# The last clamp of the hidden activation taken from ScalarE to VectorE in a state-space and quantized-FFN layer

## The chip, the cores and the metric

The kernel runs on one Trainium2 chip, on all 8 cores. Every core gets 2 of the 16 sequences (8192 tokens) and works alone: no data passes between cores. The metric is the device time in microseconds of the slowest core.

In the text, PE is TensorE, DVE is VectorE, ACT is ScalarE, SP is the engine that issues most DMAs, and PEld is the weight load that goes with each matmul.

## The reference

One layer: `x = layernorm(x + ssm(x))`, then `x = layernorm(x + ffn(x))`, with x of 16 x 4096 x 1024. The change concerns the FFN, whose activations and weights are rounded to fixed point. Cut to what matters:

```python
def fixed_quant(x, width, frac_width):
    scale = 2.0 ** frac_width
    return clip(round(x * scale), -2**(width-1), 2**(width-1) - 1) / scale
def quantized_relu(x):
    return relu(fixed_quant(x, 8, 4))
h = einsum(fixed_quant(x, 8, 4), fixed_quant(w1, 8, 6)) + fixed_quant(b1, 8, 6)
h = quantized_relu(h)            # 4096 hidden values of each token
out = einsum(fixed_quant(h, 8, 4), fixed_quant(w2, 8, 6)) + fixed_quant(b2, 8, 6)
```

The hidden value is thus scaled by 16, rounded, cut at 127 from above and at 0 from below.

## The kernel before, in words

The program has two phases, written out by hand in one function, `build_nc`. `op`, `wait` and `dma` append instructions to the list of one engine; each engine runs its list in order, and waits on counting semaphores: `tm` counts PE's finished groups, `vd` DVE's instructions, `sd` ACT's. `mm_group` emits one accumulating chain of matmuls into the next of 8 PSUM banks, taken in turn; if the bank's last reader is not done, PE waits for it there. All of a group's matmuls but the last carry line 209, the last carries line 206.

Phase A (lines 291 to 438) is the state-space layer, in 16 blocks of 512 tokens; its result goes to the DRAM tensor `r1s`. Then the FFN weights are loaded and quantized (lines 447 to 479).

Phase B (line 566 on) is the first layernorm, the FFN and the second layernorm, in 32 blocks of 256 tokens, as a software pipeline over three blocks. Iteration `it` does, in the order of each engine's list:

- for block t1 = it + 1, sums over the 1024 features of the input and of its squares on PE (lines 579 to 583). The squares, `sqb1`, were made on ACT (`emit_sq1`, line 509) at the end of the iteration before. `sqb1` lies in the same memory as `htmp8b`, so ACT waits until DVE is through with `htmp8b` (line 505), and behind its own `hq_sb` writes (line 506). `rows_and_s` (lines 518 to 537) makes mean and reciprocal deviation from the sums.
- for block t3 = it - 1, the second FFN matmul: 8 groups of 32 matmuls from `hq_sb` and `w2q`. Each group waits for the last write of `hq_sb` (line 595), and DVE adds bias and residual (line 597). Then ACT makes the squares `sqb2` (line 609), and PE sums them.
- for block t1, DVE applies the layernorm (lines 555 and 561) and quantizes to `xq_sb` (lines 636, 641, 647).
- for block t2 = it, the hidden loop (lines 682 to 723), of which the change is a part. It has 8 steps (`gsub`). In each, PE runs 4 groups of 8 matmuls (`w1q` with `xq_sb`, 128 hidden rows each). DVE makes three passes of 4 instructions over `htmp8b`, a buffer of 4 x 256 fp32 values that exists once: line 696 adds the bias, multiplies by 16 and frees the PSUM bank, line 703 rounds, line 710 takes the minimum with 127. Then ACT applies Relu in 4 instructions (line 718) and writes `hq_sb` in bf16. `prev_htmp_v` and `prev_htmp_s` hold the last DVE and ACT user of `htmp8b`; line 696 of the next step waits for both (lines 690 and 691).
- for block t3, DVE applies the second layernorm (lines 555 and 561 with `ob`), SP stores the result.

In the loop it thus reads, for one step:

```python
wait("V", "vd", prev_htmp_v[0], selfdep=True)
wait("V", "sd", prev_htmp_s[0])
...
wait("S", "vd", v)
...
prev_htmp_s[0] = hq_sd
```

Of the kernel before, what the change touches and what calls it, by code (L numbers as in the profile page):

```python
# [9 lines left out]
AF = mybir.ActivationFunctionType  # L10
ALU = mybir.AluOpType
# [23 lines left out]
def build_nc(debug=False):  # L35
# [90 lines left out]
    hq_sb = sb("hq_sb", [128, HC, TB], BF16, "B")  # L126
    r2_sb = sb("r2_sb", [128, DC, TB], BF16, "B")
    ob = sb("ob", [128, DC, TB], F32, "B")
    htmp8b = sb("htmp8b", [128, 4, TB], F32, "B")
# [16 lines left out]
    with contextlib.ExitStack() as st:  # L146
# [14 lines left out]
        def wait(eng, sem, val, force=False, selfdep=False):  # L161
            if val is None or val <= 0:
                return
            if not force and not selfdep and own_sem.get(eng) == sem:
                return
            if not force and waited[eng].get(sem, 0) >= val:
                return
            waited[eng][sem] = max(waited[eng].get(sem, 0), val)
            emit(eng, lambda E, s=sems[sem], v=val: E.wait_ge(s, v))  # L169
# [4 lines left out]
        def op(eng, fn, inc=None, inck=1):  # L174
            if inc is None:
                emit(eng, fn)
                return None
            cnt[inc] += inck
            emit(eng, lambda E, f=fn, s=sems[inc], k=inck: f(E).then_inc(s, k))
            return cnt[inc]  # L180
# [40 lines left out]
        def dma(eng, q, out_ap, in_ap, pre=()):  # L221
            for s_name, v in pre:
# [24 lines left out]
                                          scalar1=RATE_EPS, scalar2=-1.0,  # L247
                                          op0=ALU.add, op1=ALU.mult), inc="vd")
# [42 lines left out]
        for it in range(NTA + 1):  # L291
            t = it
            tp = it - 1
            if t < NTA:
# [12 lines left out]
                for e in range(8):  # L307
# [5 lines left out]
                        out=u_bf[:, p, e, :], in_=full(b)), inc="sd")  # L313
                    free_bank(b, "sd", sv)
                    u_copy_done = sv
                if debug and t == 0:
# [8 lines left out]
                    out=e1_t[:], in_=full(b), func=AF.Exp,  # L325
# [4 lines left out]
                    out=sp_t[:], in_=e1_t[:], func=AF.Ln, bias=cb_one[:]), inc="sd")  # L330
# [3 lines left out]
                    out=ld_t[:], in0=sp_t[:], scalar1=DT_MAX, scalar2=negrate[:],  # L334
                    op0=ALU.min, op1=ALU.mult), inc="vd")
                wait("S", "vd", vv)
                sv = op("S", lambda E, p=par: E.activation(
                    out=dec_t[:, p, :], in_=ld_t[:], func=AF.Exp), inc="sd")
                wait("V", "sd", sv)
                omd_vv = op("V", lambda E, p=par: E.tensor_scalar(  # L340
                    out=omd_t[:], in0=dec_t[:, p, :], scalar1=1.0, scalar2=-1.0,
                    op0=ALU.subtract, op1=ALU.mult), inc="vd")
# [3 lines left out]
                    out=c_t[:], in0=omd_t[:], in1=full(b), op=ALU.mult), inc="vd")  # L346
# [4 lines left out]
                else:  # L351
                    init = h_t[:, (t - 1) % 2, TA - 1:TA]
                scan_vd[t] = op("V", lambda E, p=par, i=init: E.tensor_tensor_scan(
                    out=h_t[:, p, :], data0=dec_t[:, p, :], data1=c_t[:],
# [3 lines left out]
                    out=hb_t[:, p, :], in_=h_t[:, p, :]), inc="vd")  # L358
# [141 lines left out]
        prev_htmp_s = [0]  # L500
# [65 lines left out]
        for it in range(-1, NTB + 1):  # L566
# [19 lines left out]
            if do3:  # L586
                p3 = t3 % 2
                st3 = state[t3]
                r2_vd = None
                mm2_groups = []  # L590
                for e in range(DC):
                    mlist = [(w2q[:, k, e * 128:(e + 1) * 128], hq_sb[:, k, :])
                             for k in range(HC)]
                    b, tv = mm_group(mlist, lambda bb: ln_slice(bb, TB),
                                     pre_waits=[("sd", st3["hq_sd"])])
                    wait("V", "tm", tv)
                    r2_vd = op("V", lambda E, b=b, e=e, p=p3: E.scalar_tensor_tensor(  # L597
                        out=r2_sb[:, e, :], in0=ln_slice(b, TB),
                        scalar=b2q[:, e:e + 1], in1=x1_sb[:, p, e, :],
                        op0=ALU.add, op1=ALU.add), inc="vd")  # L600
                    free_bank(b, "vd", r2_vd)
                    if e == 3 and do1:
                        bmb1, brs1, tvrs1 = emit_bcasts(rows1, rows1_vd, sv1)
                if not do1:
                    pass
                wait("S", "vd", r2_vd)
                sq2v = None
                for c in range(DC):
                    sq2v = op("S", lambda E, c=c: E.activation(  # L609
                        out=sqb2[:, c, :], in_=r2_sb[:, c, :], func=AF.Square),  # L610
                        inc="sd")
                bm2, tvm2 = mm_group([(ones_bf[:], r2_sb[:, c, :]) for c in range(DC)],
                                     lambda b: row_slice(b, TB),
                                     pre_waits=[("vd", r2_vd)])
                bv2, tvv2 = mm_group([(ones_bf[:], sqb2[:, c, :]) for c in range(DC)],
                                     lambda b: row_slice(b, TB),
                                     pre_waits=[("sd", sq2v)])
            elif do1:
                bmb1, brs1, tvrs1 = emit_bcasts(rows1, rows1_vd, sv1)
# [42 lines left out]
            def emit_ln2_apply(bcasts):  # L662
                bmb2, brs2, tvrs2 = bcasts
                if t3 >= 1 and out_store[t3 - 1] is not None:
                    wait("V", "qo", out_store[t3 - 1])
                src2 = [r2_sb[:, c, :] for c in range(DC)]
                dst2 = [ob[:, c, :] for c in range(DC)]
                apply2_vd = emit_apply(src2, dst2, bmb2, brs2, tvrs2)
                if debug and t3 == 0:
                    dma("Y", "qd", dbg["hq0"].rearrange("(c p) t -> p c t", p=128),  # L670
                        hq_sb[:, :, :], pre=[("sd", st3["hq_sd"])])
                colp = slice(t3 * TB, (t3 + 1) * TB)
                dstap = outT.rearrange("(c p) t -> p c t", p=128)[:, :, colp]
                out_store[t3] = dma("Y", "qo", dstap, ob[:, :, :],
                                    pre=[("vd", apply2_vd)])
# [3 lines left out]
            if do2:  # L679
                p2 = t2 % 2  # L680
                hq_vd = None
                for gsub in range(HC // 4):
                    groups = []
                    for j in range(4):
                        hc = gsub * 4 + j
                        mlist = [(w1q[:, k, hc * 128:(hc + 1) * 128],
                                  xq_sb[:, p2, k, :]) for k in range(DC)]
                        groups.append(mm_group(mlist, lambda bb: ln_slice(bb, TB),
                                               pre_waits=[("vd", state[t2]["xq_vd"])]))
                    wait("V", "vd", prev_htmp_v[0], selfdep=True)  # L690
                    wait("V", "sd", prev_htmp_s[0])
                    for j in range(4):
                        b, tv = groups[j]
                        hc = gsub * 4 + j
                        wait("V", "tm", tv)
                        v = op("V", lambda E, b=b, hc=hc, j=j: E.tensor_scalar(  # L696
                            out=htmp8b[:, j, :], in0=ln_slice(b, TB),
                            scalar1=b1q16[:, hc:hc + 1], scalar2=16.0,
                            op0=ALU.add, op1=ALU.mult), inc="vd")
                        free_bank(b, "vd", v)  # L700
                    wait("V", "vd", v, selfdep=True)
                    for j in range(4):
                        v = op("V", lambda E, j=j: E.tensor_scalar(  # L703
                            out=htmp8b[:, j, :], in0=htmp8b[:, j, :],
                            scalar1=MAGIC, scalar2=MAGIC,
                            op0=ALU.add, op1=ALU.subtract), inc="vd")
                    prev_htmp_v[0] = v
                    wait("V", "vd", v, selfdep=True)
                    for j in range(4):
                        v = op("V", lambda E, j=j: E.tensor_scalar(  # L710
                            out=htmp8b[:, j, :], in0=htmp8b[:, j, :],
                            scalar1=127.0, scalar2=None,
                            op0=ALU.min, op1=ALU.bypass), inc="vd")
                    prev_htmp_v[0] = v
                    wait("S", "vd", v)
                    for j in range(4):
                        hc = gsub * 4 + j
                        hq_sd = op("S", lambda E, j=j, hc=hc: E.activation(  # L718
                            out=hq_sb[:, hc, :], in_=htmp8b[:, j, :],
                            func=AF.Relu), inc="sd")  # L720
                    prev_htmp_s[0] = hq_sd
                    if gsub == 6 and do3:
                        ln2_bcasts = emit_ln2_rows()
                state[t2]["hq_sd"] = hq_sd
                if do3:
                    emit_ln2_apply(ln2_bcasts)
            if 0 <= it + 2 < NTB and "sq1_sd" not in state[it + 2]:
# [87 lines left out]
```

How the kernel before makes its waits and increments, by code:

```python
        def wait(eng, sem, val, force=False, selfdep=False):  # L161
            if val is None or val <= 0:
                return
            if not force and not selfdep and own_sem.get(eng) == sem:
                return
            if not force and waited[eng].get(sem, 0) >= val:
                return
            waited[eng][sem] = max(waited[eng].get(sem, 0), val)
            emit(eng, lambda E, s=sems[sem], v=val: E.wait_ge(s, v))
# [4 lines left out]
        def op(eng, fn, inc=None, inck=1):  # L174
            if inc is None:
                emit(eng, fn)
                return None
            cnt[inc] += inck
            emit(eng, lambda E, f=fn, s=sems[inc], k=inck: f(E).then_inc(s, k))
            return cnt[inc]
```

## Time and profile before

| | us |
|---|---|
| two timed runs | 3930.99 and 4051.89 |
| their median | 3991.44 |
| profiled execution | 3932.01 |
| its span on the slowest core (core 2) | 3930.4 |
| spans of the 8 cores | 3920.2 to 3930.4 |
| mean granted TensorE clock, by core | 0.905 to 0.909 of full |

The profile is one execution, read on its slowest core; the span runs from its first to its last instruction. Durations of instructions are means or single cases from it. On an engine instructions overlap: the next one starts before the end of the last, so the time that a row of the timeline gives for x4 is less than four times the mean of one.

### The profile page before, as it was taken

The page shows a single profiled execution, that of the slowest core. Times are in us where ns is not written, and L with a number is a line of the kernel's source. Part 1 is how long each engine was busy: PE and PEld are TensorE (multiplying, and loading weights), DVE is VectorE, ACT ScalarE, POOL GpSimd, SP SyncE. Part 2 cuts the span into 40 slices and gives each one's busy share as a digit, 9 for nine tenths or more (in the row PEclk, how much of TensorE's full clock was granted, in tenths as well). Part 3 has the DMA queues.
Part 4 walks back from the last instruction along what each step waited for, and adds up shares of the span by engine and source line. Part 5 has one row for each costly group of instructions (what it writes and reads, how often), then busy time and mean ns, then how long its engine had stood idle before and what let it go on. Part 6 is the DMA issues. An engine that isn't in the chain of part 4 may idle for free.

```text
span 3930.4 us, 56360 instructions; the slowest of 8 cores (3920.2 to 3930.4 us)
## 1 busy us (share of the span) xinstructions
PE 2965.1 (75%) x21120; PEld 2102.0 (53%) x21120; DVE 2016.3 (51%) x5836; ACT 786.7 (20%) x2003; POOL 19.0 (0%) x26
## 2 busy tenths in 40 slices
PE   3999999940577777777777777777777777677777
PEld 1444444410466656656555566665666666556665
DVE  0444333358555555555555555555555555555554
ACT  1222222300211121211211211112121211221111
POOL 0000000000000000000000000000000000000000
PEclk9999999975689999899988899999999988988998
DMA  7133322136000000000000000000000000000000
GB/s 105 32 47 46 47 45 43 33 118 245 22 17 17 17 17 23 17 17 17 17 17 17 22 23 17 17 17 17 22 17 17 17 17 17 17 28 17 12 12 22
DMA packets 109820, 128.16 MB, mean 33 GB/s; under 512 B 3936, under 2 KB 102240, under 8 KB 108528
## 3 DMA queue, kind: packets, MB, share of 16 engines
q1 hardware_dynamic: 71936, 83.89, 6.6%
q0 software_dynamic: 20976, 23.89, 5.1%
q10 hardware_dynamic: 16640, 16.78, 1.6%
q8 instruction: 172, 2.82, 0.3%
q14 instruction: 96, 0.79, 0.1%
HBM read 98.07 MB, written 50.33 MB: 38 GB/s over the span
## 4 chain that ended last, share of the span: by engine, by line
PE 47%; DVE 32%; ACT 11%; issue 6%; DMA 2%; another core or an unknown queue 2%; DVEq 1%; ACTq 0%; SPq 0%
PE pb L209 42%; DVE htmp8b L696 8%; ACT hq_sb L718 8%; DVE htmp8b L703 6%; DVE htmp8b L710 6%; PE pb L206 5%; DVE x_sb L561 2%; DVE x_sb L555 2%; ACT sqb L509 2%; DVE htmp8b L636 1%; DVE htmp8b L641 1%; DVE xq_sb L647 1%; DVEq L169 1%; DMA wstage_a<-w1T 1%
## 5 line engine op out<-in xcount | busy, mean ns | idle before, releaser
L209 PE MATMUL pb<-xq_sb,w1q 128*128 128x256 bf16 x7168 | 973.1, 284 | 299.6 <-DVE htmp8b L696 240.5
L209 PEld LDWEIGHTS pb<-xq_sb,w1q 128*128 128x128 bf16 x7168 | 705.4, 101 | 486.3 <-issue 384.2
L209 PE MATMUL pb<-hq_sb,w2q 128*128 128x256 bf16 x7936 | 945.3, 281 | 14.3 <-ACT hq_sb L718 14.3
L209 PEld LDWEIGHTS pb<-hq_sb,w2q 128*128 128x128 bf16 x7936 | 794.3, 101 | 150.6 <-issue 37.9
L696 DVE TENSOR_SCALAR htmp8b<-pb,b1q 128x256 f32<-128x256 f32 x1024 | 424.6, 475 | 362.4 <-ACT hq_sb L718 350.6
L597 DVE SCALAR_TENSOR_TENSOR r_sb<-pb,b2q,x_sb 128x256 bf16<-128x256 f32 x256 | 123.7, 483 | 844.2 <-PE pb L206 844.2
L718 ACT ACTIVATE hq_sb<-htmp8b 128x256 bf16<-128x256 f32 x1024 | 341.5, 404 | 987.1 <-DVE htmp8b L710 987.1
L209 PE MATMUL pb<-xb,winT_sb 128*128 128x512 bf16 x1792 | 431.0, 381 | 61.4 <-DMA xb<-xT 61.4
L209 PE MATMUL pb<-sqb,ones_bf 128*1 128x256 bf16 x448 | 96.5, 385 | 329.9 <-ACT sqb L509 278.2
L209 PEld LDWEIGHTS pb<-xb,winT_sb 128*128 128x128 bf16 x1792 | 175.0, 98 | 275.4 <-issue 69.0
L206 PE MATMUL pb<-xq_sb,w1q 128*128 128x256 bf16 x1024 | 290.4, 284 | 0.0
L609 ACT ACTIVATE sqb<-r_sb 128x256 bf16<-128x256 bf16 x256 | 81.9, 402 | 946.3 <-DVE r_sb L597 946.3
L710 DVE TENSOR_SCALAR htmp8b<-htmp8b 128x256 f32<-128x256 f32 x1024 | 230.5, 288 | 29.1 <-DVE htmp8b L703 1.8
L703 DVE TENSOR_SCALAR htmp8b<-htmp8b 128x256 f32<-128x256 f32 x1024 | 230.3, 288 | 28.5 <-DVE htmp8b L696 1.4
L209 PEld LDWEIGHTS pb<-sqb,ones_bf 128*1 128x1 bf16 x448 | 45.1, 107 | 371.6 <-issue 348.3
L209 PE MATMUL pb<-z_sb,woutT_sb 128*128 128x512 bf16 x896 | 217.0, 383 | 9.5 <-DVE z_sb L420 9.5
L388 DVE TENSOR_TENSOR r_sb<-pb,xb 128x512 bf16<-128x512 f32 x128 | 88.5, 691 | 244.5 <-PE pb L206 244.5
L209 PEld LDWEIGHTS pb<-z_sb,woutT_sb 128*128 128x128 bf16 x896 | 88.1, 98 | 117.5 <-issue 13.3
L312 ACT CAST u_bf<-pb 128x512 bf16<-128x512 f32 x128 | 74.9, 585 | 377.7 <-PE pb L206 377.7
L209 PE MATMUL pb<-r1ld,ones_bf 128*1 128x256 bf16 x224 | 36.4, 313 | 149.1 <-DMA r1ld<-r1s 147.3
L509 ACT ACTIVATE sqb<-r1ld 128x256 bf16<-128x256 bf16 x256 | 81.9, 402 | 204.5 <-DMA r1ld<-r1s 188.4
L206 PE MATMUL pb<-row,ones_row 1*128 1x256 f32 x256 | 80.2, 434 | 53.6 <-DVE htmp8b L696 50.2
(88 smaller groups left out, 1834.9 us busy)
## 6 DMA issues: line engine op xcount, KB each, us to landing
outT<-ob SPq DMA_DIRECT2D x32, 1024.0 KB, 4.4
xb<-xT POOLq DMA_DIRECT2D x16, 1024.0 KB, 16.1
r1s<-r_sb ACTq DMA_DIRECT2D x16, 1024.0 KB, 8.4
r1ld<-r1s SPq DMA_DIRECT2D x32, 512.0 KB, 4.2
wstage_a<-w1T SPq DMA_DIRECT2D x4, 2048.0 KB, 9.3
wstage_b<-w1T SPq DMA_DIRECT2D x4, 2048.0 KB, 9.5
wstage_a<-w2T SPq DMA_DIRECT2D x4, 2048.0 KB, 8.6
wstage_b<-w2T SPq DMA_DIRECT2D x4, 2048.0 KB, 8.5
```

The source lines that it names most:

```text
L206: E.matmul(o, l, r, **kw), inc="tm")
L209: E.matmul(o, l, r, **kw))
L388: vv = op("V", lambda E, b=b, e=e, p=parp, xp=tp % 3: E.tensor_tensor(out=r1_sb[:, p, e, :], in0=full(b), in1=xb[:, xp, e, :], op=ALU.add) ...
L509: sqv = op("S", lambda E, c=c, p=p: E.activation(out=sqb1[:, c, :], in_=r1ld[:, p, c, :], func=AF.Square), inc="sd")
L555: E.tensor_tensor(out=d, in0=s, in1=ln_slice(b, TB), op=ALU.subtract), inc="vd")
L561: E.tensor_tensor(out=d, in0=d, in1=ln_slice(b, TB), op=ALU.mult), inc="vd")
L597: r2_vd = op("V", lambda E, b=b, e=e, p=p3: E.scalar_tensor_tensor(out=r2_sb[:, e, :], in0=ln_slice(b, TB), scalar=b2q[:, e:e + 1], in1=x1 ...
L609: sq2v = op("S", lambda E, c=c: E.activation(out=sqb2[:, c, :], in_=r2_sb[:, c, :], func=AF.Square), inc="sd")
L696: v = op("V", lambda E, b=b, hc=hc, j=j: E.tensor_scalar(out=htmp8b[:, j, :], in0=ln_slice(b, TB), scalar1=b1q16[:, hc:hc + 1], scalar2=16 ...
L703: v = op("V", lambda E, j=j: E.tensor_scalar(out=htmp8b[:, j, :], in0=htmp8b[:, j, :], scalar1=MAGIC, scalar2=MAGIC, op0=ALU.add, op1=ALU. ...
L710: v = op("V", lambda E, j=j: E.tensor_scalar(out=htmp8b[:, j, :], in0=htmp8b[:, j, :], scalar1=127.0, scalar2=None, op0=ALU.min, op1=ALU.b ...
L718: hq_sd = op("S", lambda E, j=j, hc=hc: E.activation(out=hq_sb[:, hc, :], in_=htmp8b[:, j, :], func=AF.Relu), inc="sd")
```

## The change

The four Relu instructions on ACT (line 718) are gone from every step. DVE's third pass, which took the minimum with 127 in place in `htmp8b`, now takes the minimum with 127 and the maximum with 0 in one instruction and writes `hq_sb` in bf16. `prev_htmp_s` is no longer set in the loop, so that it holds the last `sqb1` write. The second FFN matmul waits for DVE's count in place of ACT's.

```diff
-                                     pre_waits=[("sd", st3["hq_sd"])])
+                                     pre_waits=[("vd", st3["hq_vd"])])
...
                     for j in range(4):
-                        v = op("V", lambda E, j=j: E.tensor_scalar(
-                            out=htmp8b[:, j, :], in0=htmp8b[:, j, :],
-                            scalar1=127.0, scalar2=None,
-                            op0=ALU.min, op1=ALU.bypass), inc="vd")
+                        hc = gsub * 4 + j
+                        v = op("V", lambda E, j=j, hc=hc: E.tensor_scalar(
+                            out=hq_sb[:, hc, :], in0=htmp8b[:, j, :],
+                            scalar1=127.0, scalar2=0.0,
+                            op0=ALU.min, op1=ALU.max), inc="vd")
+                    hq_sd = None
                     prev_htmp_v[0] = v
-                    wait("S", "vd", v)
-                    for j in range(4):
-                        hc = gsub * 4 + j
-                        hq_sd = op("S", lambda E, j=j, hc=hc: E.activation(
-                            out=hq_sb[:, hc, :], in_=htmp8b[:, j, :],
-                            func=AF.Relu), inc="sd")
-                    prev_htmp_s[0] = hq_sd
...
-                state[t2]["hq_sd"] = hq_sd
+                state[t2]["hq_vd"] = v
```

DVE's list at the last two steps of a hidden loop and the sums behind it, before; `pb` is a PSUM bank, `b1q` the bias, `row` a row of layernorm sums:

```order
L696 TENSOR_SCALAR htmp8b<-pb,b1q_47 128x256 x4
L703 TENSOR_SCALAR htmp8b<-htmp8b 128x256 x4
L710 TENSOR_SCALAR htmp8b<-htmp8b 128x256 x4
L518 TENSOR_SCALAR row_0_53<-pb 1x256
L523 TENSOR_TENSOR row_1_54<-row_0_53 1x256
```

The same place with the change:

```order
L696 TENSOR_SCALAR htmp8b<-pb,b1q_47 128x256 x4
L703 TENSOR_SCALAR htmp8b<-htmp8b 128x256 x4
L711 TENSOR_SCALAR hq_sb<-htmp8b 128x256 x4
L518 TENSOR_SCALAR row_0_53<-pb 1x256
L523 TENSOR_TENSOR row_1_54<-row_0_53 1x256
```

DVE has as many instructions as before, in the same order; the third pass has another output.

ACT's list from one hidden loop to the next, before; `sqb_89` is `sqb1`, `sqb_90` is `sqb2`:

```order
L718 ACTIVATE hq_sb<-htmp8b 128x256 x32
L509 ACTIVATE sqb_89<-r1ld 128x256 x8
L534 ACTIVATE row_1_54<-row_2_55,cb_eps 1x256
L537 ACTIVATE row_3_56<-row_1_54 1x256
L609 ACTIVATE sqb_90<-r_sb 128x256 x8
L534 ACTIVATE row_1_58<-row_2_59,cb_eps 1x256
L537 ACTIVATE row_3_60<-row_1_58 1x256
```

And with the change:

```order
L509 ACTIVATE sqb_89<-r1ld 128x256 x8
L534 ACTIVATE row_1_54<-row_2_55,cb_eps 1x256
L537 ACTIVATE row_3_56<-row_1_54 1x256
L609 ACTIVATE sqb_90<-r_sb 128x256 x8
L534 ACTIVATE row_1_58<-row_2_59,cb_eps 1x256
L537 ACTIVATE row_3_60<-row_1_58 1x256
```

The 32 Relu instructions of each block are gone; the rest of ACT's list stands in the same order.

## Rows read from the trace of the kernel before

**Rows 1.** The page: busy time of each engine.

```profile
PE 2965.1 (75%) x21120; PEld 2102.0 (53%) x21120; DVE 2016.3 (51%) x5836; ACT 786.7 (20%) x2003; POOL 19.0 (0%) x26
```

**Rows 2.** Waits: engine, line, whom it waited for, us in total, times, longest.

```profile
DVE htmp8b L696 <- ACT hq_sb L718: 350.6, 218, 2.0
...
PE pb L209 <- ACT sqb L509: 278.2, 32, 12.8
...
PE pb L209 <- DVE htmp8b L696: 242.3, 151, 3.2
...
PE pb L209 <- ACT hq_sb L718: 14.3, 2, 8.0
```

**Rows 3.** Timeline of one hidden-loop step: start, us, engine, instructions [idle before].

```profile
2034.88 1.66 DVE L696 TENSOR_SCALAR htmp8b<-pb,b1q 128x256 f32<-128x256 f32 x4 [1.60 <-ACT hq_sb L718]
...
2035.51 0.92 PE L209 MATMUL pb<-xq_sb,w1q 128*128 128x256 bf16 x7 [1.13 <-DVE htmp8b L696]
...
2036.64 0.90 DVE L703 TENSOR_SCALAR htmp8b<-htmp8b 128x256 f32<-128x256 f32 x4
...
2037.65 0.90 DVE L710 TENSOR_SCALAR htmp8b<-htmp8b 128x256 f32<-128x256 f32 x4
...
2038.64 1.33 ACT L718 ACTIVATE hq_sb<-htmp8b 128x256 bf16<-128x256 f32 x4 [3.94 <-DVE htmp8b L710]
...
2038.89 0.27 PE L206 MATMUL pb<-xq_sb,w1q 128*128 128x256 bf16 x1
2040.15 1.66 DVE L696 TENSOR_SCALAR htmp8b<-pb,b1q 128x256 f32<-128x256 f32 x4 [1.60 <-ACT hq_sb L718]
```

**Rows 4.** Timeline of the same block: its last step, and PE until the second matmul.

```profile
2065.90 0.42 PE L206 MATMUL pb<-r1ld,ones_bf 128*1 128x256 bf16 x1
...
2069.57 0.90 DVE L710 TENSOR_SCALAR htmp8b<-htmp8b 128x256 f32<-128x256 f32 x4
...
2070.56 1.33 ACT L718 ACTIVATE hq_sb<-htmp8b 128x256 bf16<-128x256 f32 x4 [3.94 <-DVE htmp8b L710]
2071.98 2.56 ACT L509 ACTIVATE sqb<-r1ld 128x256 bf16<-128x256 bf16 x8
2073.21 2.74 DVE L561 TENSOR_TENSOR ob<-ob,pb 128x256 f32<-128x256 f32 x8
...
2074.68 1.65 PE L209 MATMUL pb<-sqb,ones_bf 128*1 128x256 bf16 x7 [8.37 <-ACT sqb L509]
...
2076.48 5.51 PE L209 MATMUL pb<-hq_sb,w2q 128*128 128x256 bf16 x31
```

**Rows 5.** Timeline: a second-matmul group at full rate, and the one behind it.

```profile
2081.94 3.55 PE L209 MATMUL pb<-hq_sb,w2q 128*128 128x256 bf16 x31
...
2085.43 3.55 PE L209 MATMUL pb<-hq_sb,w2q 128*128 128x256 bf16 x31
```

**Rows 6.** Groups by line and form: busy, mean ns of one, idle before.

```profile
L718 ACT ACTIVATE hq_sb<-htmp8b 128x256 bf16<-128x256 f32 x1024 | 341.5, 404 | 987.1 <-DVE htmp8b L710 987.1
L710 DVE TENSOR_SCALAR htmp8b<-htmp8b 128x256 f32<-128x256 f32 x1024 | 230.5, 288 | 29.1 <-DVE htmp8b L703 1.8
...
L647 DVE TENSOR_SCALAR xq_sb<-htmp8b 128x256 bf16<-128x256 f32 x256 | 57.5, 288 | 6.8
```

**Rows 7.** Timeline: one pass of line 647, into bf16.

```profile
2024.43 0.90 DVE L647 TENSOR_SCALAR xq_sb<-htmp8b 128x256 bf16<-128x256 f32 x4
```

**Rows 8.** Windows: stretch, length, busy us of each engine (instructions), granted clock, DMA share, GB/s.

```profile
100.00:600.00 500.00, 490.96 (x2268) 220.41 (x2267) 200.65 (x307) 149.08 (x227) 8.74 (x10) 1.00 0.28 43
1300.00:3900.00 2600.00, 1964.59 (x15790) 1573.36 (x15789) 1423.64 (x4722) 501.89 (x1480) 0.00 (x0) 0.91 0.06 18
...
2021.00:2063.00 42.00, 30.23 (x254) 24.56 (x253) 29.90 (x107) 8.93 (x26) 0.00 (x0) 0.98 0.05 14
2063.00:2075.00 12.00, 3.63 (x20) 1.93 (x19) 9.87 (x35) 5.22 (x16) 0.00 (x0) 0.66 0.00 1
```

**Rows 9.** Timeline: PE's sums of the squares ten blocks earlier.

```profile
1163.03 1.65 PE L209 MATMUL pb<-sqb,ones_bf 128*1 128x256 bf16 x7 [9.08 <-ACT sqb L509]
```

More of the change, by code:

```diff
@@ L670, in emit_ln2_apply @@
                     dma("Y", "qd", dbg["hq0"].rearrange("(c p) t -> p c t", p=128),
-                        hq_sb[:, :, :], pre=[("sd", st3["hq_sd"])])
+                        hq_sb[:, :, :], pre=[("vd", st3["hq_vd"])])
                 colp = slice(t3 * TB, (t3 + 1) * TB)
```

## The prediction, as it was put on record

> **What bounds the kernel now.** I read the busy shares first. PE is busy 75% of the span, DVE 51%, ACT 20% [rows 1], so no engine is full and the time must be in waits. The list of waits comes next [rows 2]. DVE's line 696 waited for ACT's line 718 for 350.6 us in 218 cases, 1.61 us each, and PE waited for line 696 for 242.3 us: PE is held by DVE, and DVE by ACT. The third large wait, PE for the squares of line 509 (278.2 us, 32 cases, once in each block), hangs on the same chain, since ACT does these squares behind the Relus of the last step.
>
> The timeline of one step shows why [rows 3]. One step goes from line 696 at 2034.88 to line 696 at 2040.15, 5.27 us. In it line 696 takes 1.76 to the start of line 703, line 703 takes 1.01 to line 710, line 710 takes 0.99 to the Relu, and the Relu 1.51 to the next line 696. These sum to 5.27, with nothing beside one another: `htmp8b` exists once, so it is a closed ring of DVE and ACT. PE's four groups of the step run from 2035.51 to 2039.16 and are then short of banks. Each further group starts 0.87 later: a group of 32 matmuls at full rate takes 3.49 from start to start (2081.94 to 2085.43 [rows 5]), and a step also has 32. So PE needs 3.49 of the 5.27. The hidden loop is bound by the ring, and the end of the loop by the ring and then line 509.
>
> **The change, part by part.**
>
> *Relu off ACT.* 1024 instructions of line 718 go, 341.5 us of ACT's busy time [rows 6]. Busy time is not what counts; what counts is the 1.51 that the Relu puts between DVE's third pass and the next line 696.
>
> *The third pass of DVE.* The minimum of line 710 becomes minimum and maximum, written to `hq_sb` in bf16. The trace has no such instruction, but it has two neighbours: line 710 (fp32 out, one operation) and line 647 (fp32 in, bf16 out, in SBUF), both with a mean of 288 ns [rows 6], and four of either take 0.90 [rows 3, 7]. Lower bound: 0.90, since neither the output type nor an operation more shows as a cost. A gain below that is excluded, as the count of elements is the same and no row of this shape is shorter. Upper bound: the slowest four of this size that DVE has in the loop, line 696 from PSUM, 1.66 [rows 3]. I take 0.90, because line 647 is nearest: same source, same kinds of operands, same output type.
>
> *The new link.* Line 696 of the next step now waits only for DVE's own third pass (and for an old `sqb1` count, long met). From line 703 to line 710 DVE waits in the same way for itself, and there start to start is 1.01 for a pass of 0.90, a gap of 0.11. So the new step is 1.76 + 1.01 + 1.00 = 3.77, against 5.27: 1.50 saved. There are 32 blocks with 7 such links: 224 x 1.50 = 336.0 us.
>
> *Is PE late then?* PE needs 3.49 in a step of 3.77, so DVE still sets the pace, with 0.28 in hand. A bank comes free at the first instruction of line 696; PE started 0.63 after it and had its four groups done 4.28 after it [rows 3]. Their reader is line 696 two steps later, 7.54 later. So PE does not hold DVE. What is late next is DVE itself, and if PE's rate fell by more than 8% (3.77 / 3.49), PE.
>
> *The end of the loop.* Before, the third pass started at 2069.57, the Relus at 2070.56, the squares at 2071.98, and PE's sums of the squares at 2074.68, after 8.37 idle [rows 4]. Now the squares need only the end of the third pass and may start where the Relus did: 2071.98 - 2070.56 = 1.42 earlier. In the last block there are no squares, and the second matmul waits for `hq_sb` directly; it gains the same (the wait of 14.3 in 2 cases [rows 2] is of this kind). 32 x 1.42 = 45.4 us.
>
> *Does the gain stay?* Behind the squares PE runs its sums and then the second matmul without a gap [rows 4], so what is gained there moves all that follows. DVE's other work at that place is the second layernorm, which ended at 2075.95 (line 561), 1.27 behind the start of the sums. In the changed kernel DVE is 7 x 1.50 = 10.5 earlier there and PE 11.9, so the layernorm ends 2.7 behind the start of the sums. The first thing that needs DVE then is the result of the first group of the second matmul, more than 7 us behind that start, so this costs nothing. If the cover were gone it would cost at most these 1.4 us a block, 45 us. The move of the wait in line 595 from ACT's count to DVE's costs nothing: that count is met before the squares are made.
>
> *Nothing else moves.* DVE has as many instructions, no DMA changes, SP's list is the same.
>
> Sum: 336.0 + 45.4 = 381.4 us. The profiled execution had 3932.0 us in all, 1.6 more than its span, which I leave. 3932.0 - 381.4 = 3550.6, so 3551 us, 9.7% less. The two timed runs were 3930.99 and 4051.89, their median 3991.44; the profiled execution agrees with the lower, and so the forecast is to be set against runs such as that one.
>
> **Two rules weighed.** The four instructions of line 647 take 0.90 at 288 ns each [rows 6, 7], so a new one starts about every 0.20 us, before the end of the last. The Trainium skill (VectorE: DVE Perf Modes, "The DRAIN you can't avoid") says that the next instruction does not start until the pipe of the last has emptied. Taken by the durations, four would need 4 x 0.288 = 1.15 instead of 0.90, and the third pass would cost 256 x 0.25 = 64 us more, 3615 in all. Here the trace disagrees, in every pass, and the measurement decides.
>
> The granted clock is 1.00 in a stretch of phase A where PE is busy 491 of 500 us, while the other cores run the same program [rows 8]. The Trainium skill (TensorE: Matmul & The Clock Gate, Part 1) warns that with three or more cores of a die on dense matmuls a current limit lowers the die's clock to 13/16. By that rule a step would be 3.49 x 16/13 = 4.30, and PE-bound: 224 x 0.97 + 45 = 262 us saved, some 3670. By this rule, the trace disagrees in the stretch named.
>
> **The rivals.**
>
> *PE's rate falls when its loop gets denser.* One of the two runs before was 120.9 us above the other, on the same program. If the denser loop (PE needed for 3.49 of 3.77 instead of 3.49 of 5.27) calls forth such a run as the rule, the same 120.9 come on top, and PE's reserve of 8% in the loop just holds: 3551 + 121 = 3672. For it: that run. Against it: 1.00 at 98% busy [rows 8].
>
> *The clock stays at its upper level.* In the 12 us around PE's idle gap of 8.37 the granted clock is 0.66, against 0.98 in the loop ahead [rows 8], so PE comes back at 1.2 GHz: the sums take 1.80 to the second matmul, and its first group 5.62 against 3.49 [rows 4, 5]. If the shorter loop spared this, each block would gain about 2.13 + 0.85 = 3.0, 31 blocks 92 us: 3459. Against it: PE's gap is 8.37 now, and the last two links of the chain to the squares get 1.50 and 1.42 shorter, so 5.5 are left, or nearly 7 if PE does its last groups and sums ahead of it at the full rate. I expect the same fall.
>
> *The new third pass is slow.* At 1.66 in place of 0.90 a step is 4.53: 224 x 0.74 + 32 x 0.66 = 187 us saved, 3745. Only the upper bound speaks for it.
>
> *Slower: PE loses its clock inside the loop.* At the lower level the 8 matmuls of the sums took 1.80 [rows 4], 0.22 each, so 32 take about 6.9. A step would be 6.9 instead of 5.27, 224 x 1.63 - 45 = 320 us more: 4252. It decides from where more than half of the loop's matmuls run at 1.2 GHz, (5.27 - 3.49) / (6.9 - 3.49) = 0.52. Against it: the clock is 0.98 in a loop that is less dense than the new one [rows 8].
>
> **How the numbers follow.** Forecast as summed: 0.82. Lower PE rate: 0.07. Clock kept: 0.05. Slow third pass: 0.03. Slower by the clock in the loop: 0.03. The forecast's own spread is small: if the link costs 0.2 more or less it is 224 x 0.2 = 45 us. That gives 3505 below. Above I add the 64 us of a slower pass and some 15 for a clock that is a little lower in places: 3630. The four rivals with 0.18 lie outside. Faster by over 2% (2% is about what a measurement of this kernel can tell from no change) is all but the last case and some unknown: 0.96. Within 2%: 0.01. Slower by over 2%: 0.03.
>
> **What would show it.** In the changed profile: line 696 no longer waits for ACT; line 696 to line 696 is 3.77; four instructions of line 711 take 0.90 and have a mean of 288 ns; line 509 starts about 1.0 after the last third pass starts; PE's wait for line 509 is 5.5 to 7 us in each block, and its wait for line 696 in the loop falls from 1.6 to 0.3 a step. The sums of the squares of two blocks that are ten apart start 911.65 us apart [rows 4, 9], so a block takes 91.2 us; it should take 91.2 - 11.9 = 79.3. The prediction is wrong if the step is above 3.9, if line 696 waits for PE, or if the granted clock in the loop falls under 0.93, where PE is the slower one.

## The result and the profile after

The changed kernel takes 0.9052 of the time of the kernel before, with a 95% interval of 0.9038 to 0.9067: it is faster by 9.5%. The profiled execution took 3565.8 us, against 3932.0 before and 3551 forecast; the fastest of its runs was at 3558.34. The median over its 11 timed runs, 3701.18, also holds 7 in which the cores of one die had a lower granted clock and took longer (3 of 10 of the kernel before were such), and every ratio in this text leaves them out on both sides.

The page of the changed kernel, busy time of each engine:

```profile
PE 2879.2 (81%) x21120; PEld 2071.4 (58%) x21120; DVE 2016.2 (57%) x5836; ACT 445.2 (12%) x979; POOL 19.0 (1%) x26
```

Against [rows 1], ACT lost 341.5 us and 1024 instructions, and DVE's busy time is the same to 0.1 us. PE's busy time is 86 us lower (2965.1 to 2879.2) with the same 21120 matmuls: fewer of them ran at the lower clock, as the windows below show. The span is 366 us shorter (3930.4 to 3564.3), and only ACT has fewer instructions. What went was mostly waiting.

The groups by line and form of the changed kernel, with busy time, mean ns, and idle time before:

```profile
L696 DVE TENSOR_SCALAR htmp8b<-pb,b1q 128x256 f32<-128x256 f32 x1024 | 424.7, 476 | 42.7 <-DVE hq_sb L711 39.9 <-PE pb L206 2.7 <-DVE xq_sb L647 0.2
L703 DVE TENSOR_SCALAR htmp8b<-htmp8b 128x256 f32<-128x256 f32 x1024 | 230.3, 288 | 27.7 <-DVE htmp8b L696 0.5
L711 DVE TENSOR_SCALAR hq_sb<-htmp8b 128x256 bf16<-128x256 f32 x1024 | 230.3, 288 | 27.8 <-DVE htmp8b L703 0.5
```

The new third pass has a mean of 288 ns, as line 710 and line 647 had [rows 6]. The idle time ahead of line 696, 350.6 us behind ACT before [rows 2], is 42.7 in all. None of it is ACT's, 39.9 is behind line 711 and 2.7 is put down to PE. The 39.9 us are 0.18 in each of the 224 steps that follow another, as the timeline shows. Two steps of the hidden loop of the changed kernel (start, us, engine, instructions, idle before):

```profile
1989.59 1.66 DVE L696 TENSOR_SCALAR htmp8b<-pb,b1q 128x256 f32<-128x256 f32 x4 [0.18 <-DVE hq_sb L711]
...
1991.35 0.90 DVE L703 TENSOR_SCALAR htmp8b<-htmp8b 128x256 f32<-128x256 f32 x4
...
1992.35 0.90 DVE L711 TENSOR_SCALAR hq_sb<-htmp8b 128x256 bf16<-128x256 f32 x4
...
1993.43 1.66 DVE L696 TENSOR_SCALAR htmp8b<-pb,b1q 128x256 f32<-128x256 f32 x4 [0.18 <-DVE hq_sb L711]
```

The step is 3.84 or 3.85 (1989.59 to 1993.43), against 5.27 in [rows 3] and 3.77 forecast. Line 696 to 703 takes 1.76 and line 703 to 711 takes 1.00, against 1.76 and 1.01 forecast. The link from line 711 to line 696 takes 1.08 in place of 1.00: its gap is 0.18, not 0.11. This is the first thing to explain.

The end of a hidden loop of the changed kernel, in the same view:

```profile
2012.05 0.27 PE L206 MATMUL pb<-r1ld,ones_bf 128*1 128x256 bf16 x1
2012.66 1.66 DVE L696 TENSOR_SCALAR htmp8b<-pb,b1q 128x256 f32<-128x256 f32 x4 [0.18 <-DVE hq_sb L711]
...
2015.43 0.90 DVE L711 TENSOR_SCALAR hq_sb<-htmp8b 128x256 bf16<-128x256 f32 x4
...
2016.48 2.56 ACT L509 ACTIVATE sqb<-r1ld 128x256 bf16<-128x256 bf16 x8 [29.56 <-DVE hq_sb L711]
...
2019.18 1.65 PE L209 MATMUL pb<-sqb,ones_bf 128*1 128x256 bf16 x7 [6.86 <-ACT sqb L509]
...
2020.97 3.29 PE L209 MATMUL pb<-hq_sb,w2q 128*128 128x256 bf16 x23
```

Line 509 starts 1.05 after the last third pass starts; with the Relu between, it was 2.41 (2069.57 to 2071.98 [rows 4]). PE's wait for it is 6.86, where 8.37 was. And PE comes back slow as before: the sums take 1.79 to the second matmul (1.80 in [rows 4]).

The windows of the changed kernel: the long stretch, the 27 us of a loop, and PE's gap behind it. The columns are as in [rows 8]; the granted clock stands behind the five engines' busy times:

```profile
1300.00:3500.00 2200.00, 1834.55 (x15334) 1501.15 (x15335) 1376.59 (x4566) 191.48 (x550) 0.00 (x0) 0.94 0.07 20
1985.80:2012.70 26.90, 25.83 (x217) 21.51 (x215) 24.18 (x86) 0.92 (x2) 0.00 (x0) 0.96 0.01 2
2012.70:2019.00 6.30, 0.00 (x0) 0.00 (x0) 6.06 (x20) 2.52 (x8) 0.00 (x0) 0.72 0.00 0
```

PE is now busy for 25.8 of 26.9 us in the loop, and DVE nearly as long. The granted clock over the long stretch rose from 0.91 [rows 8] to 0.94, and still falls in the gap (0.72).

A block can be cut at four instants. The tables and the means in the text are over 29 of the 32 blocks (the first and the last two are left out), on the slowest core of the profiled execution. "Loop" is from the first line 696 to the last, "end" from there to the second matmul, "first group" the first of its 8 groups, "rest" all that follows up to the next loop.

| kernel | loop | end | first group | rest | block |
|---|---|---|---|---|---|
| before | 37.03 | 9.73 | 4.90 | 39.45 | 91.10 |
| changed | 26.99 | 8.33 | 4.64 | 39.49 | 79.44 |

### The profile page after: what moved, and what is told of

The parts are those of the page before. It is cut to its first block, busy times and chain, and to the rows that moved or that the text cites. A ratio compares the mean times of both kernels' runs of the same rounds, so it can differ in the third digit from the quotient of the medians.

```text
span 3564.3 us, 54880 instructions; the slowest of 8 cores (3547.9 to 3564.3 us)
## 1 busy us (share of the span) xinstructions
PE 2879.2 (81%) x21120; PEld 2071.4 (58%) x21120; DVE 2016.2 (57%) x5836; ACT 445.2 (12%) x979; POOL 19.0 (1%) x26
## 4 chain that ended last, share of the span: by engine, by line
PE 53%; DVE 33%; issue 5%; ACT 3%; DMA 2%; another core or an unknown queue 2%; DVEq 1%; ACTq 0%; SPq 0%
PE pb L209 48%; DVE htmp8b L696 9%; DVE htmp8b L703 6%; DVE hq_sb L711 6%; PE pb L206 6%; DVE x_sb L561 2%; DVE x_sb L555 2%; ACT sqb L509 2%; DVE htmp8b L636 2%; DVE htmp8b L641 2%; DVE xq_sb L647 2%; DMA wstage_a<-w1T 1%; DMA wstage_a<-w2T 1%; DVEq L169 1%
## 5 line engine op out<-in xcount | busy, mean ns | idle before, releaser
L209 PE MATMUL pb<-xq_sb,w1q 128*128 128x256 bf16 x7168 | 922.6, 275 | 119.7 <-DVE row L518 54.5
L209 PEld LDWEIGHTS pb<-xq_sb,w1q 128*128 128x128 bf16 x7168 | 687.9, 98 | 271.8 <-issue 189.5
L696 DVE TENSOR_SCALAR htmp8b<-pb,b1q 128x256 f32<-128x256 f32 x1024 | 424.7, 476 | 42.7 <-DVE hq_sb L711 39.9
L209 PE MATMUL pb<-sqb,ones_bf 128*1 128x256 bf16 x448 | 86.9, 355 | 273.4 <-ACT sqb L509 221.7
L206 PE MATMUL pb<-xq_sb,w1q 128*128 128x256 bf16 x1024 | 281.2, 275 | 0.0
L711 DVE TENSOR_SCALAR hq_sb<-htmp8b 128x256 bf16<-128x256 f32 x1024 | 230.3, 288 | 27.8 <-DVE htmp8b L703 0.5
L703 DVE TENSOR_SCALAR htmp8b<-htmp8b 128x256 f32<-128x256 f32 x1024 | 230.3, 288 | 27.7 <-DVE htmp8b L696 0.5
L333 DVE TENSOR_SCALAR ld_t<-sp_t,negrate 128x512 f32<-128x512 f32 x16 | 7.8, 486 | 204.5 <-ACT sp_t L329 204.5
L209 PEld LDWEIGHTS pb<-r1ld,ones_bf 128*1 128x1 bf16 x224 | 16.6, 85 | 166.1 <-issue 161.4
```

The lines of the kernel that those rows point to most:

```text
L206: E.matmul(o, l, r, **kw), inc="tm")
L209: E.matmul(o, l, r, **kw))
L696: v = op("V", lambda E, b=b, hc=hc, j=j: E.tensor_scalar(out=htmp8b[:, j, :], in0=ln_slice(b, TB), scalar1=b1q16[:, hc:hc + 1], scalar2=16 ...
L703: v = op("V", lambda E, j=j: E.tensor_scalar(out=htmp8b[:, j, :], in0=htmp8b[:, j, :], scalar1=MAGIC, scalar2=MAGIC, op0=ALU.add, op1=ALU. ...
L711: v = op("V", lambda E, j=j, hc=hc: E.tensor_scalar(out=hq_sb[:, hc, :], in0=htmp8b[:, j, :], scalar1=127.0, scalar2=0.0, op0=ALU.min, op1 ...
```

## The experiments

Line numbers in the rows below are those of the kernel that was run, and may be shifted by a few.

### The gap of 0.18: the order of two waits

```diff
+                    wait("V", "tm", groups[0][1])
                     wait("V", "vd", prev_htmp_v[0], selfdep=True)
                     wait("V", "sd", prev_htmp_s[0])
```

> The changed kernel, but DVE waits for PE's first group of the step before it waits for its own third pass, in place of after it. In the changed kernel line 696 to line 696 is 3.85 us, 0.07 more than forecast; all of it is the gap from line 711's end to line 696 (0.18, where 0.11 was forecast). Theory: the second wait instruction, which always stands met, is worked off behind the first and costs these 0.07. Then the gap falls to 0.11, the step to 3.77, and the time falls by 224 x 0.07 = 16 us, to about 3546 (ratio to the kernel before about 0.901). Rival: the gap belongs to line 696 itself (source in PSUM) or to line 711's other output; then gap, step and time stay: 0.18, 3.85, 3562, ratio 0.905.

Measured: 0.8978 (0.8951 to 0.9004), profiled execution 3545.2 us. DVE in the loop:

```profile
1986.94 1.66 DVE L697 TENSOR_SCALAR htmp8b<-pb,b1q 128x256 f32<-128x256 f32 x4
1988.70 0.90 DVE L704 TENSOR_SCALAR htmp8b<-htmp8b 128x256 f32<-128x256 f32 x4
1989.71 0.90 DVE L712 TENSOR_SCALAR hq_sb<-htmp8b 128x256 bf16<-128x256 f32 x4
1990.72 1.66 DVE L697 TENSOR_SCALAR htmp8b<-pb,b1q 128x256 f32<-128x256 f32 x4
```

The step is 3.78 and the gap 0.11, with the same source in PSUM and the same output. The rival falls. The ratio is lower than the 0.901 expected: a block takes 78.64 in place of 79.44, of which 0.49 is the loop (26.50), as expected, and 0.33 the first group of the second matmul (4.31 in place of 4.64), which was not.

The other way round, one more met wait was put ahead of the second pass:

```diff
                     wait("V", "vd", v, selfdep=True)
+                    wait("V", "tm", groups[0][1], force=True)
                     for j in range(4):
```

> The changed kernel with one wait instruction more per step, for a PE count that is long met, directly ahead of line 703 and behind DVE's wait for its own first pass. Theory (a met wait behind a real one costs 0.07 us): line 696 to line 703 grows from 1.76 to 1.83, the step to 3.92, the time by 256 x 0.07 = 18 us to about 3580 (ratio 0.909). Rival (the gap belongs to line 696 or to line 711's output): nothing changes, 3562, ratio 0.905.

Measured: 0.9100 (0.9080 to 0.9121). DVE in the loop:

```profile
1997.80 1.66 DVE L696 TENSOR_SCALAR htmp8b<-pb,b1q 128x256 f32<-128x256 f32 x4 [0.17 <-PE pb L206]
1999.63 0.90 DVE L704 TENSOR_SCALAR htmp8b<-htmp8b 128x256 f32<-128x256 f32 x4 [0.17 <-PE pb L206]
2000.64 0.90 DVE L712 TENSOR_SCALAR hq_sb<-htmp8b 128x256 bf16<-128x256 f32 x4
2001.71 1.66 DVE L696 TENSOR_SCALAR htmp8b<-pb,b1q 128x256 f32<-128x256 f32 x4 [0.18 <-DVE hq_sb L712]
```

Line 696 to the second pass is 1.83, where it was 1.76. The step is 3.91. So on DVE a wait that is met, but stands behind the one that ends last, costs 0.07 us here, and ahead of it costs nothing that shows. The row also names PE as the releaser, though line 696 had itself waited for that same group before it started: it is the wait behind, not PE, that shows.

### The ring or ACT's load: two buffers, Relu left on ACT

```diff
+    htmp8c = sb("htmp8c", [128, 4, TB], F32, "B", at=handles["sqb2"][1])
+    htmps = (htmp8b, htmp8c)
...
+                    hb = htmps[gsub % 2]
...
-                    wait("V", "sd", prev_htmp_s[0])
+                    wait("V", "sd", relu_sd[gsub - 2] if gsub >= 2 else prev_htmp_s[0])
```

This is the kernel before, and its three DVE passes and the Relu work on `hb`.

> The kernel before, with Relu left on ACT with all its 1024 instructions, but with two buffers in turn in place of the one htmp8b in the hidden loop. Theory: what the change gained in the loop is the opening of the ring, not the work taken off ACT. Then DVE alone sets the step: 3.85, or 3.92 if a third wait instruction adds 0.07, and line 696 waits for ACT no more; the end of the loop gets no shorter (1.42 us in each of 32 blocks, 45 us, not gained). Time 3562 + 45 = 3607, or 3623 with the third wait (ratio 0.916 to 0.920). Rival: what counted is ACT's load or its instructions; then the time stays near the kernel before, 3937 (ratio 1.00).

Measured: 0.9234 (0.9213 to 0.9255), profiled execution 3634.3 us. Its DVE and ACT in the loop:

```profile
2016.12 1.66 DVE L700 TENSOR_SCALAR htmp8b<-pb,b1q 128x256 f32<-128x256 f32 x4 [0.24 <-DVE htmp8c L714]
2017.89 0.90 DVE L707 TENSOR_SCALAR htmp8b<-htmp8b 128x256 f32<-128x256 f32 x4
2018.89 0.90 DVE L714 TENSOR_SCALAR htmp8b<-htmp8b 128x256 f32<-128x256 f32 x4
2019.89 1.33 ACT L722 ACTIVATE hq_sb<-htmp8b 128x256 bf16<-128x256 f32 x4 [2.58 <-DVE htmp8b L714]
2020.04 1.66 DVE L700 TENSOR_SCALAR htmp8c<-pb,b1q 128x256 f32<-128x256 f32 x4 [0.24 <-DVE htmp8b L714]
```

The Relu (2019.89) now runs beside the next line 696 (2020.04 here). The step is 3.92, with a gap of 0.24, which is 0.11 and two waits of 0.07 behind. ACT has all of its 1024 Relus, and yet most of the gain is there: the gain in the loop was the opening of the ring, and ACT's load cost the loop nothing beyond that third wait. Expected were 0.916 to 0.920, measured 0.923. The rest is in the first group of the second matmul, 5.28 against 4.64, which is the clock (below).

### The end of the loop: Relu on ACT in the last step only

```diff
+                    if gsub < 7:
...
+                    else:
+                        for j in range(4):
+                            v = op("V", lambda E, j=j: E.tensor_scalar(
+                                out=htmp8b[:, j, :], in0=htmp8b[:, j, :],
...
+                        wait("S", "vd", v)
+                        for j in range(4):
```

> The changed kernel with the last of the 8 steps of each hidden loop put back as before: line 710 in place and Relu on ACT. Theory: the end-of-loop term is real: the squares start 1.42 us later, all that follows too, and the time rises by 32 x 1.42 = 45 us to 3607 (ratio 0.916); the steps stay at 3.85. Rival: that 1.42 is hidden behind DVE's second layernorm or the bank waits, and the time stays at 3562 (ratio 0.905).

Measured: 0.9187 (0.9169 to 0.9205), profiled execution 3619.7 us, 54 to 57 above the changed kernel where 45 were expected. The end of its loop:

```profile
2033.79 0.90 DVE L721 TENSOR_SCALAR htmp8b<-htmp8b 128x256 f32<-128x256 f32 x4
...
2034.79 1.34 ACT L729 ACTIVATE hq_sb<-htmp8b 128x256 bf16<-128x256 f32 x4 [29.52 <-DVE htmp8b L721]
2036.21 2.56 ACT L509 ACTIVATE sqb<-r1ld 128x256 bf16<-128x256 bf16 x8
...
2038.92 1.65 PE L209 MATMUL pb<-sqb,ones_bf 128*1 128x256 bf16 x7 [8.25 <-ACT sqb L509]
```

The squares start 1.42 after the Relus, PE waits 8.25 again, and the end of the loop takes 9.71 in place of 8.33 (1.38 more). The term is real and not hidden. The first group took 5.00 in place of 4.64, which is the remaining 0.36 a block, or 11 us.

### What holds the end of the loop now

Two kernels take the squares out of the chain. The second also has the order of waits of the first experiment.

```diff
-    sqb1 = sb("sqb1", [128, DC, TB], BF16, "B", at=handles["htmp8b"][1])
     sqb2 = sb("sqb2", [128, DC, TB], BF16, "B")
+    sqb1 = sb("sqb1", [128, DC, TB], BF16, "B", at=handles["sqb2"][1])
...
-            wait("S", "vd", prev_htmp_v[0])
-            wait("S", "sd", prev_htmp_s[0], selfdep=True)
+            wait("S", "tm", sqb1_free_T[0])
...
                 p2 = t2 % 2
+                if do3:
+                    sqb1_free_T[0] = tvv2
+                if it + 2 < NTB:
+                    emit_sq1(it + 2)
```

> The changed kernel, but the squares of line 509 are made at the start of the hidden loop, into the memory of sqb2 in place of that of htmp8b, so that they no longer wait for DVE's last pass. In the changed kernel PE is idle 6.87 us for them in each block, and the second matmul starts 8.33 us after the last line 696 of the loop. Theory: behind them stands the bank of the first second-matmul group, held by the layernorm's broadcast and free only after the line 555 pass over ob, some 6.4 us after that line 696. So the second matmul starts 1.9 us earlier, PE's wait is now for DVE's line 555, PE stays idle about 5.8 us and comes back at 1.2 GHz as before: 31 x 1.9 = 58 us, 3562 becomes 3504 (ratio 0.890). Rival: no bank stands behind, and the second matmul waits only for line 711's last pass, 3.85 us after that line 696: 31 x 4.5 = 139 us, 3423 (ratio 0.869).

> e5_squares_early with the order of waits of e1_tm_wait_first. If the two gains lie in different places (step of the loop, end of the loop) they add: 16 to 20 us below e5, about 3486 (ratio 0.886). If PE's reserve in the loop is used up (PE needs 3.49 of 3.78), the step stays above 3.78 and the time at that of e5.

Measured: both 0.8945 (intervals 0.8898 to 0.8993, and 0.8906 to 0.8985). The groups of the first one say what PE waits for at the start of the second matmul:

```profile
L209 PE MATMUL pb<-hq_sb,w2q 128*128 128x256 bf16 x7936 | 963.8, 284 | 187.9 <-DVE ob L554 173.3
```

It is DVE's first layernorm pass over `ob`, which frees the bank, and the end of the loop takes 6.47 in both kernels, as the bank theory expected; its rival falls. But of the 1.86 us a block that this gained (8.33 to 6.47), 0.95 were lost in the first group, 4.64 to 5.59, and the ratio is 0.8945 where 0.890 was expected. The second kernel fits neither of the two cases written down for it. Its step did fall to 3.79 (26.50 over 7), so PE's reserve was not used up, and yet the 16 us were not added: its loop is 0.52 shorter, its first group 0.54 longer:

| kernel | loop | end | first group | rest | block |
|---|---|---|---|---|---|
| squares early | 27.02 | 6.47 | 5.59 | 39.41 | 78.49 |
| squares early, PE's wait first | 26.50 | 6.47 | 6.13 | 39.39 | 78.49 |

PE of the second kernel, from its last sums to the second matmul:

```profile
1996.16 0.27 PE L206 MATMUL pb<-sqb,ones_bf 128*1 128x256 bf16 x1
2002.36 6.17 PE L209 MATMUL pb<-hq_sb,w2q 128*128 128x256 bf16 x31 [5.92 <-DVE ob L554]
2008.36 0.27 PE L206 MATMUL pb<-hq_sb,w2q 128*128 128x256 bf16 x1
2008.47 3.55 PE L209 MATMUL pb<-hq_sb,w2q 128*128 128x256 bf16 x31
```

The first group takes 6.11 from its start to that of the next (2002.36 to 2008.47), the one behind it is at full rate. PE started earlier and ran slow for longer, by the same amount. So the instant at which the clock came back did not move with PE's start in these two kernels. The changed kernel alone shows the same from block to block. Two neighbouring blocks of it, with PE's waits all but equal:

```profile
2971.84 1.65 PE L209 MATMUL pb<-sqb,ones_bf 128*1 128x256 bf16 x7 [6.87 <-ACT sqb L509]
...
2973.63 4.00 PE L209 MATMUL pb<-hq_sb,w2q 128*128 128x256 bf16 x31
...
3050.51 1.65 PE L209 MATMUL pb<-sqb,ones_bf 128*1 128x256 bf16 x7 [6.86 <-ACT sqb L509]
...
3052.31 5.58 PE L209 MATMUL pb<-hq_sb,w2q 128*128 128x256 bf16 x31
```

Over its 29 blocks the first group takes from 3.94 to 5.58. What is saved ahead of it is therefore not always lost: in the first experiment the loop and the first group both got shorter. That left the clock as the thing to test.

### The bank

```diff
-                    if gsub == 6 and do3:
+                    if gsub == 7 and do3:
                         ln2_bcasts = emit_ln2_rows()
```

> e6 with the second layernorm's two broadcasts on PE behind the loop's last step in place of behind the seventh, so that the bank of the first second-matmul group is one that line 696 frees. Theory of e5 (bank): the second matmul now starts 3.85 us after the last line 696, 2.6 us earlier than in e6, PE's wait is for line 711: 31 x 2.6 = 81 us below e6, about 3405 (ratio 0.865). PE's idle time is then about 2 us; if that is short enough for the clock to stay at its upper level, the first group takes 3.5 in place of 5.6 and another 66 us go: 3340 (ratio 0.848). Rival of e5 (no bank): same time as e6.

Measured: 0.8673 (0.8614 to 0.8733), the fastest run at 3416.18. The end of the loop takes 3.82, as expected (3.85), and what PE waits for is line 711's pass (here L716), no longer `ob`:

```profile
L209 PE MATMUL pb<-hq_sb,w2q 128*128 128x256 bf16 x7936 | 953.3, 282 | 127.0 <-DVE hq_sb L716 127.0
```

PE was still idle for 3.97 us, twice what I expected, since I had forgotten that PE is done with its sums before the last step begins. The clock fell, and the first group takes 5.17 in the mean; in one of the 29 blocks it took 3.49 at a granted clock of 1.00, behind the same 3.97. Expected for that case was 0.865. That the number is so near is partly luck: the sum started from 3486, while the kernel that it builds on took 3524 (median of its four runs), and the time fell by 106 us (to 3416.18 and 3419.94), where 81 were expected. A block is 3.56 shorter, 2.65 at the end of the loop, as expected, and 0.96 in the first group (6.13 to 5.17), which was not.

### The clock: matmuls without use in PE's gap

Both kernels compute something that is overwritten at once, only to keep PE busy:

```diff
+            for l, rr in fill:
+                op("T", lambda E, l=l, rr=rr, b=b: E.matmul(
+                    pb[b][:, 0:TB], l, rr, start=True, stop=True))
```

In the changed kernel, ahead of the sums of the squares:

> The changed kernel with 56 matmuls without use (w1q and xq_sb, into the bank that the sums of the squares are about to overwrite) where PE is idle 6.87 us for the squares. They take 56 x 0.109 = 6.1 us and fit into the wait. Theory: PE's idle time is what lowers its clock, and the forecast's 'comes back at 1.2 GHz' costs, per block, 4.64 - 3.49 in the first second-matmul group and 1.80 - 0.98 in the sums, 1.97 us. With the filler the sums take 1.0 and the group 3.5: 31 x 1.97 = 61 us less, 3501 (ratio 0.889), and the granted clock in the gap is 1.0. Rival: the clock falls for another reason (load of the whole loop), then 3562 and 0.905, or the denser PE is slowed in the loop and the time rises.

Measured: 0.8923 (0.8906 to 0.8941), profiled execution 3515.95 us. PE and ACT at the end of the loop:

```profile
1997.53 6.29 PE L200 MATMUL pb<-xq_sb,w1q 128*128 128x256 bf16 x56
...
2001.77 2.56 ACT L512 ACTIVATE sqb<-r1ld 128x256 bf16<-128x256 bf16 x8 [29.58 <-DVE hq_sb L717]
...
2004.47 0.92 PE L212 MATMUL pb<-sqb,ones_bf 128*1 128x256 bf16 x7 [0.65 <-ACT sqb L512]
...
2005.43 3.56 PE L212 MATMUL pb<-hq_sb,w2q 128*128 128x256 bf16 x31
```

And in the windows, the long stretch, where the granted clock is 0.99, and the stretch from the added matmuls to the second matmul, where it is 1.00:

```profile
1300.00:3500.00 2200.00, 1994.99 (x17214) 1662.93 (x17212) 1403.64 (x4646) 194.02 (x558) 0.00 (x0) 0.99 0.07 21
1997.50:2005.40 7.90, 7.25 (x65) 6.01 (x64) 7.41 (x26) 2.56 (x8) 0.00 (x0) 1.00 0.01 2
```

The sums take 0.96 to the second matmul in place of 1.79, and a block 77.50 in place of 79.44: 1.94 less, with 1.97 expected. More work on PE made the kernel faster. PE's idle time is what lowers the clock here, and in the changed kernel the lower clock behind each gap costs about 2 us a block.

In the kernel with the bank moved:

> e7 with 28 such matmuls (3.05 us) ahead of the first second-matmul group, where PE is idle 3.97 us for line 711's pass. Theory: the first group takes 3.5 in place of 5.17, 31 x 1.67 = 52 us less than e7 (about 3417), so 3365, ratio 0.855. Rival as in e9: no gain, 0.867.

Measured: 0.8566 (0.8546 to 0.8587), fastest run 3369.28, profiled execution 3373.5 us, expected 3365. The end of its loop:

```profile
2010.08 1.66 DVE L707 TENSOR_SCALAR htmp8b<-pb,b1q 128x256 f32<-128x256 f32 x4
2010.71 3.22 PE L200 MATMUL pb<-xq_sb,w1q 128*128 128x256 bf16 x28 [0.78 <-DVE htmp8b L707]
...
2012.86 0.90 DVE L722 TENSOR_SCALAR hq_sb<-htmp8b 128x256 bf16<-128x256 f32 x4
...
2013.90 3.54 PE L212 MATMUL pb<-hq_sb,w2q 128*128 128x256 bf16 x31
```

The first group runs at full rate, and a block takes 73.24. This is the version that beats both kernels, the kernel before by 14.3% and the changed one by 5.2% (0.8566 / 0.9040).

The changed kernel itself was run once more beside the kernels with early squares.

> The changed kernel itself, as the reference of this series: ratio 0.905, about 3562.

Measured: 0.9040 (0.8992 to 0.9087), 3563.68 us at the median, all four runs between 3559.53 and 3564.61.

## Why the prediction was right, point by point

**The ring.** That the hidden loop was a closed ring of DVE and ACT over one buffer was right, and is shown by the two buffers: with the Relus left on ACT the step is 3.92 in place of 5.27.

**The third pass.** 0.90 for four instructions and 288 ns each, as taken from line 647. The slow third pass, as a rival, is out. The rule that the prediction takes from the Trainium skill (VectorE: DVE Perf Modes, "The DRAIN you can't avoid") would have given 1.15 by the durations, and the trace shows 0.90. The prediction read only half of it: the same section says that a next instruction that is not held starts earlier. No wait stands between the four instructions of this pass, so 0.90 does not speak against the section as a whole.

**The new link.** This step failed in its size. I took the gap from line 703 to line 710 (0.11), where DVE has one wait. Ahead of line 696 it has two, and the second, for PE's first group of the step, is one that the prediction does not name. Measured 0.18, so a step of 3.85 in place of 3.77, and a term of 224 x 1.42 = 318 us in place of 336.0. The two wait experiments show the cause in both directions.

**PE's reserve.** Right: of the 42.7 us that line 696 waits, 39.9 are behind its own engine. PE needs 3.49 of 3.85. PE's waits for line 696 ahead of the loop's matmuls fell from 242.3 us in 151 cases to 40.6 in 92, which is 0.18 for each of the 224 steps, where the prediction put 0.3. The first experiment, at 3.78, did not meet a limit either.

**The end of the loop.** Forecast 45.4 us. The end takes 8.33 in place of 9.73, so 1.40 x 32 = 45. Putting back the last step gives 1.38 a block. Right, and not hidden. PE's wait for the squares is 6.86, inside the 5.5 to 7 that the prediction gave.

**Nothing else moves.** Not quite: the first group of the second matmul takes 4.64 in place of 4.90, because the clock came back earlier in some blocks. That is 0.26 x 31 = 8 us that I had not counted, and it is luck: the same mean is 4.31 in one of the later kernels and 4.96 in another, with loops that differ from this one by 0.5 and 0.4.

**The sum.** 318 + 45 + 8 = 371 us from the first loop on, where the prediction had 381. The miss of 18 in the links is thus partly covered by the 8 that were not foreseen. Measured from the first line 696 of the first loop to the end of the span: 3930.4 - 1026.29 = 2904.1 before, 3564.3 - 1032.94 = 2531.4 after, a difference of 372.7. The two instants are these, first of the kernel before, then of the changed one:

```profile
1026.29 0.88 DVE L696 TENSOR_SCALAR htmp8b<-pb,b1q 128x256 f32<-128x256 f32 x2 [0.17 <-DVE xq_sb L647]
```

```profile
1032.94 1.27 DVE L696 TENSOR_SCALAR htmp8b<-pb,b1q 128x256 f32<-128x256 f32 x3 [0.18 <-DVE xq_sb L647]
```

Over the whole span the difference is 366.1, since the changed kernel's first loop started 6.65 us later: that much was lost ahead of it, in a part of the program that the change doesn't touch. In the later kernels this start lay between 1018 and 1040, so it differs from one execution to the next; what sets it was not tried.

**The rivals.** That the denser loop lowers PE's rate as the rule is not what the runs show: a group takes 0.87 as before, and the four runs of the repeat lie within 5 us of each other. That the clock stays up was rightly held unlikely, since a gap of 6.9 us remained; the filler kernels show what it would have been worth, 1.94 a block. The forecast for that case was 3.0 a block, because I took the one block in the rows (first group 5.62) for all; the mean was 4.90.

## What to carry to other kernels

Where two engines work in turn on one buffer, add up the links of the ring and not the busy times: each engine can be half idle and still set the pace, and a second buffer opens the ring in the loop nearly as well as moving the work does (a step of 3.92 against 3.85), though not the chain behind the loop. Put the wait that ends last behind the others, since on DVE each met wait behind it was paid here. And where PE has a gap in each block, price it together with the slow matmuls behind it: time saved ahead of a gap can be lost in them, in part or whole, and PE work without use in the gap can pay.

## What was not expected of the hardware

- A wait on a semaphore that is met long since costs DVE 0.07 us if it stands behind the wait that ends last (gaps of 0.11, 0.18 and 0.24 with none, one and two of them), and nothing that shows ahead of it (0.11).
- The instant at which PE's clock returns to its upper level is not set by when PE starts again: in the two kernels with early squares a loop shorter by 0.52 us was followed by a first group longer by 0.54, and both blocks took 78.49. In the changed kernel alone the first group took from 3.94 to 5.58 behind waits of 6.9. The Trainium skill (TensorE: Matmul & The Clock Gate, Part 1) says that the clock gate observes on a time base of its own that a kernel's start does not reset, and these kernels agree with that.
- Keeping PE busy with 56 matmuls without use took the granted clock of the long stretch from 0.94 to 0.99 and 1.94 us off each block.
